# Epilogue and norm by groups of tiles across four engines, and a gather that confirms one group back: a GNN kernel on one core

## The reference, cut to what matters

```python
x = _layernorm(x + relu((norm * x[src] summed by dst) @ W + b))          # layer 0
x = _layernorm(x + relu(x @ U.T + (x[src] summed by dst) @ V.T))         # layer 1
x = _layernorm(x + (concat(mean of x[src] by dst, x) @ W.T + b))         # layer 2
# layer 3: for each edge, over endpoints src and dst
h = relu(concat(x[src], x[dst]) @ W1 + b1)
interaction = h @ W2 + b2
gated = interaction * sigmoid(interaction @ Wg + bg)
x = _layernorm(x + (gated summed by src) / max(count, 1))
```

## Time and profile before

| | us |
|---|---|
| Median of 3 runs | 4346.5 (4345.19 to 4351.81) |
| The profiled execution's own time | 4350.17 |
| Its span | 4348.5 |
| PE busy in the span | 3556.6 (82%) |
| DVE busy | 2406.2 (55%) |
| ACT busy | 1737.0 (40%) |
| POOL busy | 1572.0 (36%) |
| Mean granted TensorE clock (1.0 is 2.4 GHz) | 0.884 |

### The profile page before, as it was taken

The page is one execution under the profiler, slowest core; times in us unless marked ns, Lnnn a source line. Parts: engine busy times, 40 slices in busy tenths (PEclk is TensorE's granted clock), DMA queues, the critical chain, the costliest instruction groups (busy, mean ns, idle before and its releaser), DMA issues.

```text
span 4348.5 us, 127519 instructions
## 1 busy us (share of the span) xinstructions
PE 3556.6 (82%) x39375; PEld 2769.1 (64%) x39376; DVE 2406.2 (55%) x6624; ACT 1737.0 (40%) x3826; POOL 1572.0 (36%) x1730
## 2 busy tenths in 40 slices
PE   5785257777777797998986999989888999899986
PEld 2343233333333697997985787777777877787775
DVE  8999989999999503205024344334433434443444
ACT  5774047777777300001002344333333433333332
POOL 2000010000000000000006777777777777777774
PEclk9887579999989898999997789888998989988897
DMA  1000012222222696896962222222222222222222
GB/s 44 3 4 1 29 66 89 89 103 89 89 89 103 237 343 245 318 341 225 341 223 54 51 57 58 56 54 56 55 55 52 59 54 56 56 54 55 56 56 41
DMA packets 186859, 446.38 MB, mean 103 GB/s; under 512 B 52907, under 2 KB 115379, under 8 KB 180271
## 3 DMA queue, kind: packets, MB, share of 16 engines
q1 hardware_dynamic: 133263, 388.80, 26.1%
q0 software_dynamic: 51328, 54.71, 6.1%
q10 hardware_dynamic: 2208, 2.10, 0.2%
HBM read 357.45 MB, written 87.99 MB: 102 GB/s over the span
## 4 chain that ended last, share of the span: by engine, by line
PE 38%; DVE 18%; DMA 13%; issue 12%; POOL 10%; ACT 3%; POOLq 2%; ACTq 1%; DVEq 1%; SPq 0%; PEldq 0%
PE ps L1448 10%; POOL x L996 10%; DVE x L509 9%; PE ps L1423 8%; DMA x<-b_table,gidx 7%; DMA rows<-adjacency 6%; PE ps L1543 5%; PE ps L1533 5%; PE ps L1555 5%; PE ps L1530 4%; DVE rows L709 4%; POOLq L990 2%; ACT ps L1175 1%; ACT stage L1194 1%; PE ps L1330 1%
## 5 line engine op out<-in xcount | busy, mean ns | idle before, releaser
L996 POOL DMA_INDIRECT x<-b_table,gidx x1568 | 1501.3, 957 | 464.2 <-issue 379.3
L1423 PE MATMUL ps<-rows 128*128 128x448 bf16 x2272 | 643.5, 420 | 227.7 <-DVE rows L709 98.1
L1448 PE MATMUL ps<-x,rows 128*128 x22050 | 684.0, 194 | 63.5 <-DMA rows<-adjacency 29.9
L709 DVE TENSOR_SCALAR rows<-iota_c,x 128x448 bf16<-128x448 bf16 x2272 | 727.6, 526 | 2.2 <-PE ps L1423 2.2
L1448 PEld LDWEIGHTS ps<-x,rows 128*128 128x128 bf16 x22050 | 666.9, 98 | 81.0 <-issue 71.1
L857 DVE TENSOR_TENSOR x<-x,ps 128x256 f32<-128x256 f32 x440 | 185.3, 421 | 937.9 <-ACT x L1261 937.2
L1423 PEld LDWEIGHTS ps<-rows 128*128 128x128 bf16 x2272 | 331.7, 146 | 539.5 <-issue 418.6
L1543 PE MATMUL ps<-w2cat,x 65*128 65x128 f32 x3520 | 561.1, 307 | 0.0
L1533 PEld LDWEIGHTS ps<-ident,x 128*64 128x64 f32 x3520 | 480.3, 156 | 104.8 <-issue 39.9
L1555 PE MATMUL ps<-x 128*128 128x65 f32 x3520 | 497.1, 289 | 60.4 <-DVE x L857 59.9
L1533 PE MATMUL ps<-ident,x 128*64 128x128 f32 x3520 | 531.3, 301 | 0.0
(11 more groups left out here) (278 smaller groups left out, 2509.4 us busy)
## 6 DMA issues: line engine op xcount, KB each, us to landing
rows<-adjacency SPq DMA_DIRECT2D x150, 800.0 KB, 6.3
rows<-adjacency SPq DMA_DIRECT2D x150, 768.0 KB, 6.1
adjacency<-stage SPq DMA_DIRECT2D x50, 1568.0 KB, 5.1
x<-src_rows SPq DMA_DIRECT2D x440, 128.0 KB
x<-b_table,gidx POOLq DMA_INDIRECT x1568
key_rows<-x ACTq DMA_DIRECT2D x1, 1024.0 KB, 4.1
pair_rows<-x ACTq DMA_DIRECT2D x1, 1024.0 KB, 7.6
pair_rows<-x SPq DMA_DIRECT2D x1, 1024.0 KB, 5.4
```

What stands on the lines that cost most here:

```text
L709: ins = e.tensor_scalar(hot_dst[:, k, :], iota_c[:], rel_col[:, bass.ds(i0 + k, 1)], digit_col[:, bass.ds(i0 + k, 1)], ALU.is_equal, ALU.mult)
L996: e.indirect_dma_start(out=BGT[:, s, j, :], out_offset=None, in_=b_table, in_offset=bass.IndirectOffsetOnAxis(ap=gidx[:, s * G + j:s * G + ...
L1423: e.matmul(psf[:, bass.ds(at_bank, WIN)], hot_src[:, k // HOTS, :, k % HOTS], hot_dst[:, k % HOTS, :], start=False, stop=False, skip_group ...
L1448: ins = e.matmul(acc_ps[:, t, :], rows[:, h, c:c + P], x3[:, bass.ds(2 * pr + h // 2, 1), k * D:(k + 1) * D] .rearrange("p a f -> p (a f)" ...
```

## The change

Six edits:

1. The centring leaves DVE. For each group DVE makes the negative mean (`sum_rows`), POOL adds it and squares (`centre`, with its own semaphore between the two), and DVE sums the squares two groups later (`sum_squares`).
2. Variance, root and reciprocal come in two parts in layers 0 and 1 (`ROOT`: tiles 0 to 31, 32 to 49). The first part is made behind group 5; the second behind the first split group of the next layer. The last two sums of squares move there too.
3. Layer 2's epilogue has the turning of `X` and the b product inside the loop over groups, on centred rows that aren't normalised yet; DVE scales the product by the row's inverse deviation while taking it out of PSUM (`b_rows`). Variance and root go by single groups. The bias is added to `X` ahead of time, into `T1`. The products of part a come after, and are split by groups of 512 columns with a scratch of their own (`rest_a`), so that DVE waits for no DMA. ACT normalises `X` itself, in 50 instructions of 64 columns, and clears `total`.
4. `b_table` is stored in three DMAs (32, 16 and 2 tiles).
5. `GLAG` is 1, and the wait and the confirmation stand ahead of the fourth indirect DMA of a group in place of ahead of its first.
6. The last norm goes by groups of tiles, with POOL's centring, two roots, and output chunks of 32 tiles and the rest.

```diff
-GLAG = 2
+GLAG = 1
+ROOT = [0, 32, NTP]
...
+            def sum_rows(layer, g):
+                t0, t1 = group_tiles(g)
+                mean = stat[:, 0, t0:t1]
+                e.wait_ge(dve, q.n)
+                q.link(e.tensor_reduce(mean, X[:, t0:t1, :], AX_X, ALU.add))
+                q.mark(f"mean{layer}_{g}", e.tensor_scalar(mean, mean, -1.0 / D, None, ALU.mult))
+            def sum_squares(layer, g):
+                t0, t1 = group_tiles(g)
+                e.wait_ge(centred, 2 * (layer * EG + g) + 2)
+                q.done(e.tensor_reduce(stat[:, 1, t0:t1], T1[:, t0:t1, :], AX_X, ALU.add))
...
+                        normalise(t0, t1)
+                        e.wait_ge(dve, q.n)
+                    split(X if layer else T1, t0, t1, AGG[:, t0:t1, :])
                     if g < EG - 1:
                         e.sem_inc(pairs_split, 4)
+                    if layer and g == 0:
+                        sum_squares(layer - 1, EG - 2)
+                        sum_squares(layer - 1, EG - 1)
+                        variance(f"var{layer - 1}_1", ROOT[1], NTP)
...
+                if layer == 2:
+                    q.link(e.tensor_tensor(T1[:], X[:], bias[:, 1, :].unsqueeze(1).to_broadcast([P, NTP, D]), ALU.add))
...
+                def b_rows(g):
+                    t0, t1 = group_tiles(g)
+                    inverse_root(5 + g, t0, t1)
+                    e.wait_ge(pair_product, g + 1)
+                    q.mark(f"p_{g}", e.tensor_tensor(
+                        AGG[:, t0:t1, :], ps[:, 6 + g % 2, 0:(t1 - t0) * D].rearrange("p (t f) -> p t f", f=D),
+                        over_f(stat[:, 0, t0:t1]), ALU.mult))
...
+                    sum_rows(layer, g)
+                    if layer < 2:
+                        if g >= 2:
+                            sum_squares(layer, g - 2)
+                        if g == EG - 2:
+                            variance(f"var{layer}_0", 0, ROOT[1])
+                    else:
+                        if g >= 2:
+                            sum_squares(2, g - 2)
+                            variance(f"var2_{g - 2}", *group_tiles(g - 2))
+                        if g >= 3:
+                            b_rows(g - 3)
...
+            for g in range(EG):
+                t0, t1 = group_tiles(g)
+                e.wait_ge(pair_product, EG + g + 1)
+                q.mark(f"a_{g}", e.tensor_tensor(
+                    T1[:, t0:t1, :], ps[:, g % 4, 0:(t1 - t0) * D].rearrange("p (t f) -> p t f", f=D),
+                    over_f(stat[:, 0, t0:t1]), ALU.mult))
+                e.wait_ge(dve, q.n)
+                split(T1, t0, t1, rest_a[:, g % 2, 0:t1 - t0, :])
...
         # POOL
+            def centre(layer, g):
+                n = layer * EG + g
+                t0, t1 = 8 * g, min(8 * g + 8, NTP)
+                xs = X[:, t0:t1, :]
+                e.wait_ge(dve, mark[f"mean{layer}_{g}"])
+                e.tensor_tensor(xs, xs, over_f(stat[:, 0, t0:t1]), ALU.add).then_inc(centred, 1)
+                e.wait_ge(centred, 2 * n + 1)
+                e.tensor_tensor(T1[:, t0:t1, :], xs, xs, ALU.mult).then_inc(centred, 1)
...
-                if not first or s >= GLAG:
-                    e.wait_ge(b_landed[(s - GLAG) % RING], 16 * G * (rnd + (s >= GLAG)))
-                    e.sem_inc(groups_landed, 1)
-                if s == GLAG - 1 and not first:
+                if s == GLAG and not first:
                     keep_ids(g - s + HALF_RING, 1)
-                if s == HALF_RING + GLAG - 1:
+                if s == HALF_RING + GLAG:
                     keep_ids(g - s + RING, 0)
...
                 for j in range(G):
+                    if j == G - 1 and (not first or s >= GLAG):
+                        e.wait_ge(b_landed[(s - GLAG) % RING], 16 * G * (rnd + (s >= GLAG)))
+                        e.sem_inc(groups_landed, 1)
                     e.indirect_dma_start(
...
         # SP
+            for lo, hi, ready in ((0, 32, "p_3"), (32, 48, "p_5"), (48, NTP, "p_6")):
+                e.wait_ge(dve, mark[ready])
+                e.dma_start(b_tiles[:, lo:hi, :], AGG[:, lo:hi, :]).then_inc(table_out, 16)
...
         # PE, layer 2, inside the loop over g
+                    if layer == 2:
+                        if g >= 1:
+                            turn_pairs(g - 1)
+                        if g >= 2:
+                            b_products(g - 2)
...
+            turn_pairs(EG - 1)
+            b_products(EG - 2)
+            b_products(EG - 1)
             for g in range(EG):
+                pair_products(g, g % 4, 0)
```

More of the change, by code:

```diff
@@ L797, in _ @@
                     xs = X[:, t0:t1, :]
-                    if layer == 1:
+                    if layer == 0:
+                        q.link(e.tensor_tensor(T1[:, t0:t1, :], o,
+                                               bias[:, 0, :].unsqueeze(1).to_broadcast([P, t1 - t0, D]), ALU.add))
+                        q.done(e.scalar_tensor_tensor(out=xs, in0=T1[:, t0:t1, :], scalar=0.0, in1=xs,
+                                                      op0=ALU.max, op1=ALU.add))
+                    elif layer == 1:
@@ L825, in _ @@
-            e.wait_ge(dve, q.n)
-            mark["b_rows"] = q.n
-            e.wait_ge(table_out, 32)
-            split(T1, 0, NTP)
-            q.done(e.memset(total, 0.0))
+                        q.done(e.tensor_tensor(xs, o, T1[:, t0:t1, :], ALU.add))
+                    mark[f"out{layer}_{g}"] = q.n
+                    sum_rows(layer, g)
[10 more added lines that the diff above has]
+                            b_rows(g - 3)
@@ L890, in _ @@
             q.link(e.reciprocal(scale[:, 2, :], stat[:, 0, :]))
[L891 to L899 removed]
+            e.wait_ge(x2_ready, 1)
+            for g in range(EG):
+                t0, t1 = group_tiles(g)
+                q.link(e.tensor_tensor(AGG[:, t0:t1, :], total[:, t0:t1, 0:D], over_f(scale[:, 2, t0:t1]), ALU.mult))
+                q.done(e.tensor_tensor(X[:, t0:t1, :], X[:, t0:t1, :], AGG[:, t0:t1, :], ALU.add))
+                sum_rows(3, g)
+                if g >= 2:
+                    sum_squares(3, g - 2)
+                if g == EG - 2:
+                    variance("var3_0", 0, ROOT[1])
+            sum_squares(3, EG - 2)
+            inverse_root(5 + EG, 0, ROOT[1])
+            mark["first_rows"] = normalise(0, ROOT[1])
+            sum_squares(3, EG - 1)
+            variance("var3_1", ROOT[1], NTP)
+            inverse_root(6 + EG, ROOT[1], NTP)
+            mark["final"] = normalise(ROOT[1], NTP)
         @block.gpsimd
@@ L1010, in _ @@
                 e.sem_inc(groups_landed, 1)
+            for g in range(EG):
+                centre(3, g)
         @block.sync
@@ L1278, in _ @@
             gate(ITEMS - 1, (ITEMS - 1) % 2, False)
-            e.wait_ge(dve, mark["var3"])
-            e.activation(stat[:, 2, :], stat[:, 1, :], ACT.Sqrt).then_inc(root_ready, 1)
+            for half in range(2):
+                root(f"var3_{half}", ROOT[half], ROOT[half + 1])
         @block.tensor
```

175 lines of the change are left out of this document (89 added, 86 removed).

## The result

| | before | after |
|---|---|---|
| Median, us | 4346.68 (4345.19 to 4351.81, 4 runs) | 4305.85 (4300.18 to 4310.72, 4 runs) |
| Ratio to before | 1 | 0.990, 95% interval 0.9881 to 0.9919 |
| Profiled execution, us | 4350.17 | 4310.72 |

What follows compares the result with a forecast made beforehand. No single engine was taken to bound the span, and POOL's rate to set the edge stage; terms 11 + 9 + 19.5 + 7 + 0 + 0 = 46.5 us took the median from 4346.5 to 4300, range 4287 to 4319.

Steps and rivals of the forecast that it cites:

- Layer 0: Layer 0's epilogue: DVE's group falls from 4.6 to 3.1 us; 12.0 saved, less 1.0 for contention, gives 11.
- Layer 1: Layer 1's epilogue: DVE's group, 2.4 us, falls under PE's 2.66; 9.9 saved, less 0.9 for contention, gives 9.
- Layer 2: Layer 2's epilogue to the table's landing: PE sets 4.0 us per group, rows ready 20.0 earlier, less 0.5: 19.5.
- Start of the edge stage: POOL's first transfers: 10.0 us lost before beside DVE's wide steps, 3 lost with short pieces, so 7 gained.
- One group back: Edge stage: confirmation already comes at the landing, so moving it one group forward gains 0; the wait has slack.
- Last norm: Final norm: ready at 4339.7 against 4340.4, 1.5 added for contention, about 1 less for the last chunk: 0 us.
- Contention eats part: Rival, chance 0.17: POOL's adds and DVE's two-input instructions take strict turns; 33.5 us saved, 4313 (or 20.5, 4326).
- PE at 1.2 GHz: Rival, chance 0.06: slow clock in layer 2's epilogue, a group costs 7.6 us, not 4.0; 14 more: 4314.
- The starved POOL: Rival, chance 0.05: the new wait ahead of each fourth transfer delays POOL; at 0.2 us per group 78 lost, 4378.
- It doesn't overlap: Rival, chance 0.03: a missed wait chains POOL, DVE and PE in the epilogues; only 7 us won, 4339.5, or nothing.
- signs of being right: POOL 5.0 us per group, idle at most 0.3, ACT waiting some 580; layers at 1731.4, 1993; first transfer 2271, none over 3.
- signs of being wrong: Idle before fourth transfers ended by landings; POOL's TENSOR_TENSOR over 1.6 us; DVE awaiting POOL before squares' sums; last norm over 36.

Runs made afterwards that it cites:

- experiment 4: Kernel after with layer 0's biased product left in PSUM instead of T1: 4303.58 us, ratio 0.9904 to the kernel before; layer 0's epilogue 26.80 against 31.61.
- Experiments 2 and 3: 2: kernel before with part a split in 7 pieces of 512 columns, 4336.13 us, ratio 0.9975; 3: kernel after with one-piece split, 4314.11 us, ratio 0.9922.
- experiment 1: Kernel before with edit 5 alone (confirmation one group back, wait ahead of the fourth transfer): 4348.29 against 4349.56 us, ratio 0.9994.
- Experiment 8: Kernel after with the wait for the group one back ahead of the second transfer instead of the fourth: 4871.14 us in one run, 565 slower.

## Why the prediction was right, and where it was off

The forecast of 4300 lies 5.9 under the median of 4305.85, inside its range, and its mechanism held. By its steps:

- *Layer 0: 9.3 for 11.* DVE's group, forecast at 3.1, took 3.71. The mis-sized term is the 1.0 for contention: experiment 4 removes it and gains 3.9. That the stage came out near the forecast all the same is because the sum without contention was too low: from DVE's first bias step to PE's restart the kernel before takes 35.68 and experiment 4 takes 22.44, 13.2 less where I had 12.0 (a group takes 2.85, not 3.1). The errors of 2.9 and 1.2 partly cancel, by luck.
- *Layer 1: 9.5 for 9.* Here the residual step has its other input in PSUM and PE's rate was the bound, as the step said; the 0.9 for contention was too much by about half.
- *Layer 2: 18.2 for 19.5.* Rows ready were to be 20.0 earlier and are, within 0.1: 2304.54 - 2249.18 = 55.4 before, 2271.99 - 2236.54 = 35.5 after. PE's group was to take 4.0 and does. The failed step is "the first two [stores], already under way, need about the same 4.65". The rows of group 3, which the first store waits for, come three groups late, so SP issued it at 2268.63, only 3.4 us ahead of the last rows, where the kernel before had 4.5. The second was issued only 0.4 ahead of them:

```profile
2271.62 4.74 SPq L1157 DMA_DIRECT2D b_table<-AGG  x2
```

The chain has the last store from 2273.19, 1.2 behind its rows, when SP was done with issuing the second, and it takes 5.18. So the table was there 6.4 after the last rows, not 4.7. The last store lands 2.6 to 3.7 after the large one in all profiles of either kernel and their variants; that it queues behind it fits this, and was only argued.
- *Start of the edge stage: 9.2 for 7.* "I take 3 lost" measured 0.8. Experiments 2 and 3 put the same 8.5 to 9.2 on the width of DVE's instructions alone, from both sides.
- *One group back: 0 for 0*, by experiment 1. Experiment 8 shows that this was the position's doing.
- *Last norm: -2.8 for 0.* The failed step is the 1.5 for contention. The two additions at the head of each group went from 0.69 each to 1.16 and 1.41, 1.2 more per group and some 7 in all, which alone would have made it about -5. As in layer 0 the price of a group without collisions was too high, 3.1 for 2.85, which gave 2 back. The working has slips too, none of which moves the sum by a microsecond: a group has four wide steps, which make the 19.4, and not "5 wide"; the last chunk is 16 tiles for 23, not 17 for 24. And the best bounds of the range add to 59, not 59.5.
- *The end of the edge stage*, 2.4 for 0, and the untouched stages, -6.2 together, are no part of the sum. Without them the touched stages gave 9.3 + 9.5 + 18.2 + 9.2 - 0.1 - 2.8 = 43.3 of 46.5.

The rivals. *Contention eats part* is real in two of its four places, layer 0 and the last norm; its price in layer 0, 1 more than my 1.0, was still under the measured 3.9, in the last norm its -3 was what the stage lost, and in layer 1 and at the edge stage's start little of it came. Strict turns are nearly, not quite, what the rows show: 1.57 where they would make 1.71. The rule of the Trainium skill named beside it (SBUF — State Buffer, Who interferes with whom) draws this line where the runs put it for DVE and POOL arithmetic: two SBUF inputs collide, one PSUM input doesn't (0.69 against 1.57). The forecast had applied it to all steps alike. *PE at 1.2 GHz* didn't come: the groups of layer 2 follow at 3.99. *The starved POOL* didn't come at the fourth transfer. *It doesn't overlap* didn't come.

Of the signs of being right, POOL's rate (with one idle time of 1.1), ACT's 571.0 us and the transfers (longest 1.28) came. The next layers began at 1737.30 and 1999.70, for 1731.4 and 1993, and the first transfer at 2279.51, for 2271; the three untouched stages ahead of it were 6.2 longer in this execution, which is most of that. Of the signs of being wrong one came: the last norm took over 36 us. POOL's TENSOR_TENSOR took at most 1.41, and DVE never waited for POOL ahead of a sum of squares.

## What to carry to other kernels

Work given to an idle engine should be priced by what it does to the instruction beside it: here POOL's steps are free beside DVE's sums and beside DVE steps that read PSUM, and cost DVE 0.35 to 0.9 us beside those that read two SBUF tiles, so it is worth moving one operand to PSUM. Wide DVE casts and subtractions stretched POOL's indirect transfers from 0.94 to as much as 5.31 us, and cutting them into pieces of 512 columns, without moving any work, gave 9 us. A confirmation belongs as far behind the last issue as its queue's next stop allows: the same wait cost nothing at the fourth transfer and 1.4 us per group at the second.

## What the runs showed of the hardware that I had not expected

- A collision costs the later instruction most of what the earlier one has left, whichever engine is late. DVE's L830 grew by 0.88 where POOL had 1.02 left (at 1719.72) and by 0.35 where it had 0.49 left (1716.54); POOL's square grew by 0.33 where L830 had 0.47 left (1717.11).
- Where POOL's queue really stopped for a landing, the next transfer began 0.73 after it (experiment 8, 3009.63); where it found the landing already there, the gap was the usual 0.30.
- A tiny DVE instruction of one SBUF input grows too: the variance's `tensor_scalar` (L750, 128 x 8) took 0.53 beside a step of POOL (at 2259.58) and 0.17 alone (at 2267.60).
- Two chips differ by 20% on the same program (4349 against 5212 us), with a granted clock of 0.89 against 0.70 in the edge stage, and so in what bounds it.
